# Layer 0 of a graph network: one tile in eight made by selection on TensorE instead of gathered by GpSimd

## The chip, the core and the metric

One core of a Trainium2 chip. The metric is the device time of one launch in microseconds; a kernel's time is the median of its runs. All times below of single instructions, waits and stretches come from one profiled execution.

## What is computed

A graph network of two layers on 12,500 nodes with 32 features and 212,500 edges, which are sorted by destination. Layer 0 is the part that the change touches:

```python
h = jnp.maximum(_layernorm(x, axis=-1), 0.0)
# layer 0
norm_src = rsqrt(maximum(deg_out, 1.0)); norm_dst = rsqrt(maximum(deg_in, 1.0))
h = features * norm_src[:, None]
msgs = h[src]
agg = segment_sum(msgs, dst) * norm_dst[:, None]
x = x + relu(agg @ weight + bias)
# layer 1: messages of h[src], a small network of edge_attr_32 and edge_attr_4, segment_sum over dst
```

`h[src]` is the row of 32 floats of the source node of every edge.

## The kernel before

The edges are padded to 208 chunks of 1024, a chunk being 8 tiles of 128 edges (one edge per partition). A row of a node's features is fetched by its index: one indirect DMA of GpSimd (L350) gathers the 128 rows of one tile from a table in DRAM into `g[:, j, t, 0:32]`. The tile `g` is a ring of four chunks (`RING` = 4, slot `j`); `idx` holds the indices of four chunks, which SP reloads once a slot's gather has landed (`load1`).

**Start.** Source digits are turned into one-hot tiles by VectorE (L738, bf16) and counted by 16 bf16 matmuls per batch on TensorE (L499), between one lone matmul at L493 and one at L505; that is the histogram, which gives the degrees. Meanwhile GpSimd gathers the raw rows of x for the first 32 chunks (the early chunks), which ScalarE keeps in SBUF (L406). Then VectorE makes layer 0's table `hn` (normalised rows times the norm), and ScalarE's queue stores it as `table1`. VectorE then makes the bounds of each chunk: the first destination row and the span of rows, in `row_i`.

**First stage of layer 0** (`beside_early`, 16 iterations). Six units alternate by the table `UNITS`: gathered, gathered, early, gathered, gathered, early. So four chunks gathered from `table1` and two early chunks are worked in an iteration. In both kinds of unit VectorE compares destinations into a one-hot tile (L783), TensorE multiplies it with the eight tiles of rows into a window of 68 destination rows (`take`, L515: eight fp32 matmuls, which the trace shows as 16 records), and VectorE adds the window to the accumulator `acc_a` (L795). TensorE's take number n waits until VectorE's take number n - 1 has added (the semaphore `opened`, L875 in VectorE's queue). Before an early chunk, VectorE splits its sources into digits and compares them (`early_onehots`, L830, L833, L835, then L840 to L847 on the rows kept), TensorE selects the norms with eight fp32 matmuls (`early_norms`, L537), and VectorE picks and applies them (`early_rows`, L856, L860, L862).

The order within a unit is written out by hand. VectorE: digits of the next unit if that is an early one, one-hot of the next unit, early rows if this is an early unit, then the addition of this unit's take. TensorE: norms if the next unit is early, wait for this unit's rows, take.

**Second stage** (`alone`, 28 iterations of four gathered chunks): one-hot of the next chunk, take of this one, and where destinations of a block of 512 nodes are complete, `mid_block` finishes the block (25 in all). GpSimd may gather into a slot again when the one-hot tile two units after the slot's use has been made (`used_in`).

**Layer 2 stage.** From 2205 us on, the second layer: gathers of all 208 chunks from `table2` run beside a long chain of matmuls and products (L605, L617, L982 to L1007). Its order is not touched.

Of the kernel before, what the change touches and what calls it, by code (L numbers as in the profile page):

```python
# [26 lines left out]
ALU = mybir.AluOpType  # L27
# [36 lines left out]
MW = 56  # L64


def gnn_program(nc, x_rows, src_all, src_chunks, src_rows, dst_all, dst_chunks, edge_t, sh_chunks,
# [3 lines left out]
    with ExitStack() as ctx:  # L71
# [11 lines left out]
        W_BANK, H_BANK, S_BANK = 0, 4, 6  # L83
# [10 lines left out]
        bound = sb("bound", [P, 2, CHUNKS])  # L94
# [16 lines left out]
        ident = sb("ident", [P, P])  # L111
        w_l0_s = sb("w_l0_s", [FEAT + 1, FEAT + 1])
# [22 lines left out]

        dst_i, src_i, src_p, src_b, src_r = (acc_a[:, k * T_ALL:(k + 1) * T_ALL].bitcast(I32) for k in range(5))
# [9 lines left out]
        early_r = early_r_all[:, 0:TILES * NR].rearrange("p (t r) -> p t r", r=NR)  # L146
        flat_q = q[:, :, :, :].rearrange("p b t k -> p (b t k)")
# [28 lines left out]
        mid_ready = sem("mid_ready")  # L176

# [76 lines left out]
        GATH = 16 * TILES  # L254
# [5 lines left out]
        def _(sp):  # L260
# [19 lines left out]
            def load1(i):  # L280
                for j in range(RING):

                    sp.wait_ge(gathered[j], GATH * (i + 1))
                    sp.dma_start(idx[:, j, :], load_from(src_chunks, RING * i + RING + j)).then_inc(idx_in[j], 16)

            def load_from(dram, c):
                return dram[c] if isinstance(c, int) else dram[bass.ds(c, 1)].rearrange("a p k -> (a p) k")

            with sp.Fori(0, EARLY_ITERS - 1) as i:
                load1(i)  # L290
# [9 lines left out]
            with sp.Fori(EARLY_ITERS - 1, ITERS - 1) as i:  # L300
                load1(i)

            for j in range(RING):
                sp.wait_ge(gathered[j], GATH * ITERS)
                sp.dma_start(idx[:, j, :], src_chunks[j]).then_inc(idx_in[j], 16)
                sp.dma_start(sh[:, j, :, :], sh_chunks[j].rearrange("p (t d) -> p t d", d=4)).then_inc(sh_in[j], 16)
# [10 lines left out]
            with sp.Fori(0, ITERS - 1) as i:  # L317
                final = final_blocks(sp, RING * i + (LOOK - 1))
                for j in range(RING):
# [4 lines left out]
                    sp.wait_ge(gathered[j], GATH * (i + ITERS + 1))  # L324
# [11 lines left out]
        def _(pool):  # L336
# [5 lines left out]
            def gather(i, table, iteration, free):  # L342

                for j in range(RING):
# [4 lines left out]
                    for t in range(TILES):  # L349
# [24 lines left out]
            gather(EARLY_ITERS, table1, EARLY_ITERS, kept_four_before)  # L374
            beside = used_in(0, len(UNITS), [UNITS.index((0, j)) for j in range(RING)])
            alone = used_in(A_UNITS, RING, range(RING))
            with pool.Fori(0, A_ITERS) as i:
                gather(i, table1, i + (EARLY_ITERS + 1), beside(i))
            with pool.Fori(0, REG_ITERS - A_ITERS - 1) as i:
                gather(i, table1, i + (EARLY_ITERS + 1 + A_ITERS), alone(i))  # L380
# [15 lines left out]
        def _(act):  # L396
# [60 lines left out]
            def coefs(i, j):  # L457
# [4 lines left out]
                act.wait_ge(gathered[j], GATH * (i + ITERS + 1))  # L462
# [24 lines left out]
        def _(pe):  # L487
# [52 lines left out]

            def beside_early(i):
                for pos, (is_early, k) in enumerate(UNITS):
# [4 lines left out]
                    else:  # L547
                        if UNITS[(pos + 1) % len(UNITS)][0]:
                            early_norms(2 * i + UNITS[pos + 1][1])
                        pe.wait_ge(gathered[k], GATH * (i + (EARLY_ITERS + 1)))  # L550
                        take(n, RING * i + (EARLY + k), k, pos % 2, lambda t: g[:, k, t, :])

            def alone(i):
                for j in range(RING):
                    pe.wait_ge(gathered[j], GATH * (i + (EARLY_ITERS + 1)))
# [15 lines left out]
            pe.wait_ge(acc_a_clear, 1)  # L571
            beside_early(0)
# [3 lines left out]
            with pe.Fori(A_ITERS, REG_ITERS) as i:  # L576
                alone(i)
            other_blocks(pe, blocks1, mid_block)
# [83 lines left out]
        def _(dve):  # L662
# [53 lines left out]
            for iota, m in ((iota_p, P), (iota_r, NR)):  # L716
# [12 lines left out]
                                          op0=ALU.bitwise_and, op1=ALU.bitwise_or))  # L729
            link(dve.tensor_copy(dig_p, src_p))  # L730
# [13 lines left out]
            with dve.Fori(1, HBATCH // 2) as i:  # L744
# [9 lines left out]
                                     op0=ALU.max, op1=ALU.mult).then_inc(table1_ready, 1)  # L754

# [69 lines left out]

            def early_onehots(e):
# [50 lines left out]
            def beside_early(i):  # L877

                for pos, (is_early, k) in enumerate(UNITS):
# [6 lines left out]
                    if is_early:  # L886
                        early_rows(2 * i + k)
                    take(len(UNITS) * i + pos, 2 * i + k if is_early else RING * i + (EARLY + k), pos % 2)

            def alone(i):  # L890
                for j in range(RING):
                    if not (isinstance(i, int) and j == RING - 1):
                        make_onehot(RING * i + (EARLY + j + 1), 1 - j % 2, onehot1_ready)
                    if j == LOOK:
# [46 lines left out]

            make_onehot(EARLY, 0, onehot1_ready)
            beside_early(0)
# [192 lines left out]
```

## Time and profile before

| | |
|---|---|
| median of 3 runs | 4374.91 us (4372.59 to 4389.63) |
| profiled execution, its own time | 4370.72 us |
| its span, first to last instruction | 4368.9 us |
| busy: TensorE / VectorE / ScalarE / GpSimd | 68% / 64% / 16% / 76% |
| mean granted TensorE clock | 0.77 |
| first take of a gathered chunk | 403.6 us |
| first stage / second stage / layer 2 | 403.6 to 1069.5 / to 2181.4 / 2205 to the end |

The granted clock is 1.00 at 2.4 GHz and 0.50 at 1.2 GHz. A gather is listed with its busy time; the rest of its spacing stands as "issue", time in which the engine waited for nothing that the profile shows.

### The profile page before, as it was taken

The page shows a single profiled execution, that of the slowest core. Times are in us where ns is not written, and L with a number is a line of the kernel's source. Part 1 is how long each engine was busy: PE and PEld are TensorE (multiplying, and loading weights), DVE is VectorE, ACT ScalarE, POOL GpSimd, SP SyncE. Part 2 cuts the span into 40 slices and gives each one's busy share as a digit, 9 for nine tenths or more (in the row PEclk, how much of TensorE's full clock was granted, in tenths as well). Part 3 has the DMA queues.
Part 4 walks back from the last instruction along what each step waited for, and adds up shares of the span by engine and source line. Part 5 has one row for each costly group of instructions (what it writes and reads, how often), then busy time and mean ns, then how long its engine had stood idle before and what let it go on. Part 6 is the DMA issues. An engine that isn't in the chain of part 4 may idle for free.

```text
span 4368.9 us, 66165 instructions
## 1 busy us (share of the span) xinstructions
PE 2966.2 (68%) x17022; PEld 2220.1 (51%) x17023; DVE 2776.1 (64%) x4667; ACT 718.6 (16%) x2399; POOL 3313.5 (76%) x3337
## 2 busy tenths in 40 slices
PE   6993444444222222222279999999999999999998
PEld 5772344434222222211256666666666666666666
DVE  7775444343222222211179999999999999899997
ACT  0000000000000000000043333333333333233322
POOL 7777777777777777777777777777777777777775
PEclk9999655555555555555599999999999999899998
DMA  2002111111111010110111111111111111111111
GB/s 51 11 11 44 37 37 42 37 37 28 15 15 15 15 15 15 15 14 14 15 27 29 29 29 28 29 29 28 29 29 27 29 28 28 27 29 29 27 29 19
DMA packets 224085, 113.80 MB, mean 26 GB/s; under 512 B 148848, under 2 KB 212145, under 8 KB 223953
## 3 DMA queue, kind: packets, MB, share of 16 engines
q0 software_dynamic: 106496, 54.74, 8.6%
q1 hardware_dynamic: 106281, 39.22, 4.0%
q10 hardware_dynamic: 11280, 19.53, 1.4%
q8 instruction: 10, 0.16, 0.0%
q14 instruction: 18, 0.15, 0.0%
HBM read 108.30 MB, written 4.92 MB: 26 GB/s over the span
## 4 chain that ended last, share of the span: by engine, by line
POOL 61%; issue 23%; PE 6%; DVE 5%; DMA 2%; ACT 1%; DVEq 1%; POOLq 1%; SPq 0%; ACTq 0%
POOL g L350 61%; PE ps L515 2%; DMA g<-table,idx 2%; PE ps L567 1%; PE ps L617 1%; PE ps L605 1%; ACT q L466 1%; DVE onehot L783 1%; ACT acc_b L445 0%; DVE prod_b L982 0%; PE ps L651 0%; DVE hn L936 0%; PE ps L653 0%; DVE ef L919 0%; ACT root L429 0%
## 5 line engine op out<-in xcount | busy, mean ns | idle before, releaser
L350 POOL DMA_INDIRECT g<-table,idx x3072 | 2990.3, 973 | 945.9 <-issue 924.2
L515 PE MATMUL ps<-onehot,g 128*33 128x68 f32 x2816 | 352.3, 318 | 986.3 <-issue 954.2
L617 PE MATMUL ps<-w_s,hid 128*128 128x256 f32 x3328 | 899.7, 417 | 2.0 <-DVE prod_a L993 1.4
L617 PEld LDWEIGHTS ps<-w_s,hid 128*128 128x128 f32 x3328 | 643.9, 204 | 454.9 <-issue 368.0
L515 PEld LDWEIGHTS ps<-onehot,g 128*33 128x33 f32 x2816 | 309.3, 174 | 1026.7 <-issue 998.4
L998 DVE TENSOR_REDUCE msg_b<-prod_b 128x128 f32<-128x1024 f32 x416 | 828.4, 1991 | 0.0
L795 DVE TENSOR_TENSOR acc_a<-acc_a,ps 33x68 f32 (+1 forms) x416 | 90.3, 217 | 1106.9 <-PE ps L515 1081.5
L605 PE MATMUL ps<-ef,w_s 32*64 32x512 f32 x832 | 482.6, 662 | 6.4 <-issue 6.3
L454 ACT ACTIVATE hid<-ps,b_s 64x512 f32<-64x512 f32 x416 | 282.2, 678 | 1118.2 <-PE ps L605 1117.8
L515 PEld LDWEIGHTS ps<-onehot,prod_a 128*128 128x128 f32 x3328 | 400.6, 193 | 119.4 <-issue 111.9
L515 PE MATMUL ps<-onehot,prod_a 128*128 128x68 f32 x3328 | 407.4, 276 | 77.4 <-issue 67.5
L466 ACT ACTIVATE q<-g,sh 128x32 f32<-128x32 f32 x1664 | 374.6, 308 | 330.8 <-DMA g<-table,idx 330.5
L982 DVE TENSOR_TENSOR prod_b<-ps,q 128x768 f32<-128x768 f32 x416 | 394.7, 949 | 20.5 <-PE ps L617 20.5
L350 POOL DMA_INDIRECT g<-x_rows,idx x256 | 309.8, 1210 | 80.1 <-issue 77.7
L783 DVE TENSOR_TENSOR onehot<-iota_all,dst_rel 128x544 f32<-128x544 f32 x416 | 300.1, 722 | 61.6 <-issue 53.3
L499 PE MATMUL ps<-acc_b 128*128 128x100 bf16 x1664 | 313.6, 370 | 33.4 <-DVE acc_b L738 33.4
L429 ACT ACTIVATE root<-stat 128x4 f32<-128x4 f32 x50 | 10.3, 205 | 1796.3 <-DVEq L689 1796.3
L499 PEld LDWEIGHTS ps<-acc_b 128*128 128x128 bf16 x1664 | 246.3, 148 | 100.4 <-DVE acc_b L738 33.6
L993 DVE TENSOR_TENSOR prod_a<-ps,q 128x512 f32<-128x512 f32 x416 | 283.6, 682 | 0.0
L515 PE MATMUL ps<-onehot,msg_b 128*56 128x68 f32 x3328 | 250.6, 231 | 0.0
L515 PEld LDWEIGHTS ps<-onehot,msg_b 128*56 128x56 f32 x3328 | 219.0, 134 | 15.1
L738 DVE TENSOR_TENSOR acc_b<-prod_a,msg_b 128x2048 bf16<-128x2048 bf16 x104 | 127.5, 1226 | 90.9 <-PE ps L499 90.9
(108 smaller groups left out, 1885.0 us busy)
## 6 DMA issues: line engine op xcount, KB each, us to landing
g<-table,idx POOLq DMA_INDIRECT x3072
ef<-edge_t SPq DMA_DIRECT2D x208, 128.0 KB
ef<-src_rows ACTq DMA_DIRECT2D x31, 512.0 KB, 3.7
idx<-src_chunks SPq DMA_DIRECT2D x416, 4.0 KB
g<-x_rows,idx POOLq DMA_INDIRECT x256
sh<-sh_chunks SPq DMA_DIRECT2D x208, 16.0 KB
table<-hn ACTq DMA_DIRECT2D x1, 1600.0 KB, 9.1
table<-hn ACTq DMA_DIRECT2D x25, 64.0 KB, 1.6
```

The costliest lines, as they stand in the source:

```text
L350: pool.indirect_dma_start(out=g[:, j, t, 0:FEAT], out_offset=None, in_=table, in_offset=bass.IndirectOffsetOnAxis(ap=idx[:, j, t:t + 1], a ...
L454: act.activation(hid[0:HID, h, :], ps[0:HID, H_BANK + h, :], ACT.Relu, bias=b1_s[:, 0:1]).then_inc(hidden_ready, 1)
L466: act.activation(q[:, j % 2, t, 8:40], g[:, j, t, 0:FEAT], ACT.Copy, scale=sh[:, j, t, 0:1])
L499: mm = pe.matmul(deg, oh_p[:, b, :, t], oh_r[:, b, :, t], start=False, stop=False, skip_group_check=True)
L515: mm = pe.matmul(ps[0:m, S_BANK + b, col:col + WIN], r, oh(t), start=(t == 0), stop=(t == TILES - 1))
L605: pe.matmul(ps[0:HID, H_BANK + h, :], w1_s[32 * j:32 * j + 32, :], ef[32 * j:32 * j + 32, 512 * h:512 * h + 512], start=True, stop=True, t ...
L617: mm = pe.matmul(w_ps[h][:, t, :], hid[:, h, P * t:P * t + P], w2_s[:, :], start=True, stop=True)
L738: ins = dve.tensor_tensor(oh[:, b, :, :], iota, dig[:, None, bass.ds(n * HB, HB)].to_broadcast([P, m, HB]), ALU.is_equal)
L783: dve.tensor_tensor(onehot[:, b, :, :], iota_all[:, None, 0:WIN].to_broadcast([P, TILES, WIN]), dst_rel[:, bass.ds(c * TILES, TILES)][:, : ...
L982: dve.tensor_tensor(prod_b[:, h, :, 0:3, :].rearrange("p t m (i o) -> p t m i o", o=MUL), w[:, :, 128:192].rearrange("p t (i o) -> p t i o ...
L993: dve.tensor_tensor(prod_a[:, b, 4 * h:4 * h + 4, :].rearrange("p t (k o) -> p t k o", o=MUL), w[:, :, 0:128].rearrange("p t (k o) -> p t ...
L998: dve.tensor_reduce(msg_b[:, b, 4 * h:4 * h + 4, 0:32].rearrange("p t (g o) -> p t g o", o=MUL), prod_b[:, h, :, :, :].rearrange("p t g (i ...
```

## The change

In layer 0, tile 7 of each of the 176 chunks that are gathered from `table1` is no longer gathered. GpSimd issues seven indirect DMAs per chunk there (`TAKEN` = 7); the 32 early chunks and layer 2 keep eight. The eighth tile is made as follows.

- Once, after the table is stored: SP loads `table1` back into SBUF as `whole` (node n lies on partition (n / 16) mod 128, in group n / 2048, at place n mod 16), and VectorE splits it into three bf16 parts whose sum is exact (`split`).
- Per chunk, SP loads the tile's 128 source indices, broadcast to all partitions (`load_key`, 64 KB). VectorE shifts them right by 4 (`key`) and compares them with the partition and group numbers into a bf16 one-hot tile of 7 x 128 columns (`make_source`).
- TensorE multiplies this with the three parts, 7 groups x 3 parts = 21 bf16 matmuls of 512 columns, into one PSUM bank (`source_rows`): for each edge the 16 rows that share its upper digits.
- VectorE picks the one of 16 (`choose`: a comparison with the low digit times the rows, 512 elements, then a sum over 16) and writes it to `g[:, j, 7, 0:32]`.

The one-hot tile of chunk m + 2 and the selection of chunk m + 1 are made in unit m. The tile `bound` and the third part lie in free space of `xc`, the semaphore targets count seven gathers in layer 0's stages, and constants are made at the start.

```diff
@@ gpsimd @@
-            def gather(i, table, iteration, free):
+            def gather(i, table, iteration, free, tiles=TILES):
...
-                    for t in range(TILES):
+                    for t in range(tiles):
...
-            gather(EARLY_ITERS, table1, EARLY_ITERS, kept_four_before)
+            gather(EARLY_ITERS, table1, EARLY_ITERS, kept_four_before, TAKEN)
...
@@ sync @@
+            def load_key(c, j):
+                row = src_rows[c:c + 1, MADE * P:] if isinstance(c, int) else src_rows[bass.ds(c, 1), MADE * P:]
+                sp.dma_start(keys[:, j, :], row.to_broadcast([P, P])).then_inc(keys_in[j], 16)
...
+                    sp.wait_ge(key_ready, RING * i + (j + 1))
+                    load_key(RING * i + (EARLY + RING + j), j)
...
+            load0(EARLY_ITERS - 1)
+            sp.wait_ge(table1_out, 16)
+            full = GROUPS - 1
+            sp.dma_start(whole[:, 0:full, :], table1[0:full * P * GROUP, :].rearrange(
+                "(k p b) f -> p k (b f)", p=P, b=GROUP)).then_inc(whole_in, 16)
...
@@ tensor @@
+            def source_rows(m, j):
+                if isinstance(m, int) and m >= M_UNITS:
+                    return
+                pe.wait_ge(source_ready, m + 1)
+                wait(pe, row_made, m - 1)
+                for k in range(GROUPS):
+                    for n in range(3):
+                        mm = pe.matmul(ps[:, R_BANK + j % 2, :], source[:, j % 2, k, :], split[n][:, k, :],
+                                       start=(k == 0 and n == 0), stop=(k == GROUPS - 1 and n == 2))
+                mm.then_inc(rows_psum, 1)
...
                         if UNITS[(pos + 1) % len(UNITS)][0]:
                             early_norms(2 * i + UNITS[pos + 1][1])
-                        pe.wait_ge(gathered[k], GATH * (i + (EARLY_ITERS + 1)))
+                        source_rows(RING * i + (k + 1), k + 1)
+                        pe.wait_ge(gathered[k], landed1(i))
+                        pe.wait_ge(row_made, RING * i + (k + 1))
                         take(n, RING * i + (EARLY + k), k, pos % 2, lambda t: g[:, k, t, :])
...
@@ vector @@
+            def make_source(m, j):
...
+                dve.wait_ge(keys_in[j], 4 * m + (16 - 4 * j))
+                wait(dve, source_ready, m)
+                dve.tensor_scalar(key, keys[:, j, :], GROUP_LOG, None, ALU.logical_shift_right).then_inc(key_ready, 1)
+                dve.wait_ge(key_ready, m + 1)
+                dve.tensor_tensor(source[:, j % 2, :, :], key[:, None, :].to_broadcast([P, GROUPS, P]),
+                                  first[:, :, None].to_broadcast([P, GROUPS, P]),
+                                  ALU.is_equal).then_inc(source_ready, 1)
+            def choose(m, j, c):
...
+                dve.wait_ge(rows_psum, m + 1)
+                dve.scalar_tensor_tensor(
+                    out=chosen.rearrange("p f b -> p b f"),
+                    in0=iota_all[:, 0:GROUP, None].to_broadcast([P, GROUP, FEAT]), scalar=low[:, bass.ds(c, 1)],
+                    in1=ps[:, R_BANK + j % 2, :].rearrange("p (b f) -> p b f", f=FEAT),
+                    op0=ALU.is_equal, op1=ALU.mult).then_inc(chosen_ready, 1)
+                dve.wait_ge(chosen_ready, m + 1)
+                dve.tensor_reduce(g[:, j, MADE, 0:FEAT], chosen, AX, ALU.add).then_inc(row_made, 1)
+            def next_rows(i, j):
+                make_source(RING * i + (j + 2), j + 2)
+                choose(RING * i + (j + 1), j + 1, RING * i + (EARLY + j + 1))
...
                     if is_early:
                         early_rows(2 * i + k)
+                    else:
+                        next_rows(i, k)
                     take(len(UNITS) * i + pos, 2 * i + k if is_early else RING * i + (EARLY + k), pos % 2)
...
+            dve.wait_ge(whole_in, 32)
+            link(dve.tensor_copy(split[0], whole))
+            link(dve.tensor_tensor(whole, whole, split[0], ALU.subtract))
+            link(dve.tensor_copy(split[1], whole))
+            dve.tensor_tensor(split[2], whole, split[1], ALU.subtract).then_inc(split_ready, 1)
```

How the order moves, first on TensorE, in the second gathered unit of an iteration (its next unit is an early one). Before, from the norms to the take (`hid` holds the early digits' one-hot, `row_i` the bounds):

```order
L537 MATMUL ps<-norm_src,hid 128x100 [waits early_p_ready]
L537 MATMUL ps<-norm_src,hid 128x100 x7
L521 TENSOR_LOAD row_i [waits onehot1_ready,gathered1]
...
L515 MATMUL ps<-onehot,g 33x68 [waits opened0]
L515 MATMUL ps<-onehot,g 33x68 x7
```

With the change (`prod_a` holds the source one-hot tile, `split_s` and `xc` the three parts):

```order
L599 MATMUL ps<-norm_src,hid 128x100 [waits early_p_ready]
L599 MATMUL ps<-norm_src,hid 128x100 x7
L611 MATMUL ps<-split_s,prod_a 128x512 [waits row_made,source_ready]
L611 MATMUL ps<-split_s,prod_a 128x512
L611 MATMUL ps<-xc,prod_a 128x512
...
L583 TENSOR_LOAD row_i [waits onehot1_ready,row_made,gathered1]
...
L577 MATMUL ps<-onehot,g 33x68 [waits opened0]
L577 MATMUL ps<-onehot,g 33x68 x7
```

The 21 matmuls for the next gathered chunk stand between the norms and the take, so the take of this chunk is queued behind them. The second place is VectorE in the same unit, from the last of the early digits' operations to the addition. Before:

```order
L847 TENSOR_TENSOR q<-q 128x256 [waits early_chain]
L783 TENSOR_TENSOR onehot<-iota_all,dst_rel 128x544
L799 TENSOR_LOAD row_i
...
L795 ISA [waits added1,seg1_done]
L795 TENSOR_TENSOR acc_a<-acc_a,ps 33x68
```

With the change:

```order
L966 TENSOR_TENSOR q<-q 128x256 [waits early_chain]
L870 TENSOR_TENSOR onehot<-iota_all,dst_rel 128x544
L920 TENSOR_SCALAR prod_a<-prod_a 128x128 [waits source_ready,keys_in3]
L922 TENSOR_TENSOR prod_a<-prod_a,first 128x896 [waits key_ready]
L932 SCALAR_TENSOR_TENSOR prod_a<-iota_all,low,ps 128x16x32 [waits rows_psum]
L938 TENSOR_REDUCE g<-prod_a 128x32 [waits chosen_ready]
L886 TENSOR_LOAD row_i
...
L882 ISA [waits added1,seg1_done]
L882 TENSOR_TENSOR acc_a<-acc_a,ps 33x68
```

The addition of this unit's take, and with it everything of the next unit, now stands behind a selection that waits for TensorE's 21 matmuls (`rows_psum`).

## Rows read from the trace of the kernel before

**Rows 1.** The page: busy times, clock in 40 slices, chain that ended last by line.

```profile
PE 2966.2 (68%) x17022; PEld 2220.1 (51%) x17023; DVE 2776.1 (64%) x4667; ACT 718.6 (16%) x2399; POOL 3313.5 (76%) x3337
PEclk9999655555555555555599999999999999899998
POOL g L350 61%; PE ps L515 2%; DMA g<-table,idx 2%; PE ps L567 1%; PE ps L617 1%; PE ps L605 1%; ACT q L466 1%; DVE onehot L783 1%; ACT acc_b L445 0%; DVE prod_b L982 0%; PE ps L651 0%; DVE hn L936 0%; PE ps L653 0%; DVE ef L919 0%; ACT root L429 0%
```

**Rows 2.** Table by stages: us, each engine's busy us (instructions), granted clock, DMA share, GB/s.

```profile
403.60:1069.50 665.90, 308.94 (x2049) 277.66 (x2049) 277.64 (x543) 0.00 (x0) 509.70 (x513) 0.57 0.16 38
1069.50:2181.40 1111.90, 273.81 (x1968) 243.33 (x1968) 241.00 (x846) 9.86 (x48) 842.21 (x887) 0.50 0.10 15
2205.00:4369.00 2164.00, 2062.63 (x11305) 1447.37 (x11304) 1971.80 (x2991) 691.05 (x2311) 1628.41 (x1664) 0.93 0.15 28
```

**Rows 3.** Timeline of GpSimd, second stage: start us, us, engine, line, operation [idle before].

```profile
1499.79 0.94 POOL L350 DMA_INDIRECT g<-table,idx  x1 [0.30 <-issue]
```

**Rows 4.** Timeline of TensorE: the first takes of the two stages.

```profile
403.63 2.02 PE L515 MATMUL ps<-onehot,g 128*33 128x68 f32 x16 [54.60 <-issue]
1069.49 2.02 PE L515 MATMUL ps<-onehot,g 128*33 128x68 f32 x16 [0.87 <-DVEq L875]
```

**Rows 5.** Timeline, first stage: half an iteration on TensorE and VectorE.

```profile
664.35 2.02 PE L515 MATMUL ps<-onehot,g 128*33 128x68 f32 x16 [2.53 <-issue]
666.59 0.22 DVE L795 TENSOR_TENSOR acc_a<-acc_a,ps 33x68 f32 x1 [5.71 <-PE ps L515]
671.46 2.02 PE L515 MATMUL ps<-onehot,q 128*33 128x68 f32 x16 [5.09 <-issue]
674.33 2.02 PE L515 MATMUL ps<-onehot,g 128*33 128x68 f32 x16 [0.85 <-DVEq L875]
678.53 3.74 PE L537 MATMUL ps<-norm_src,hid 128*128 128x100 f32 x16 [2.18 <-DVE hid L833]
```

**Rows 6.** Groups by line, shapes apart, one late addition, one DMA: prices for added operations.

```profile
L835 DVE TENSOR_TENSOR msg_b<-iota_all,acc_b 128x800 f32<-128x800 f32 x32 | 31.5, 984 | 0.0
L843 DVE TENSOR_REDUCE q<-q 128x8 f32<-128x256 f32 x32 | 13.4, 420 | 1.1
L993 DVE TENSOR_TENSOR prod_a<-ps,q 128x512 f32<-128x512 f32 x416 | 283.6, 682 | 0.0
1535.69 0.22 DVE L795 TENSOR_TENSOR acc_a<-acc_a,ps 33x68 f32 x1 [1.06 <-issue]
table<-hn ACTq DMA_DIRECT2D x1, 1600.0 KB, 9.1
```

**Rows 7.** The histogram: its matmuls, the lone ones before and after, a gather beside it.

```profile
304.70 20.52 PE L499 MATMUL ps<-acc_b 128*128 128x100 bf16 x108
L493 PE MATMUL ps<-acc_b 128*128 128x100 bf16 x1 | 0.3, 264 | 1.7 <-DVE acc_b L711 1.7
L505 PE MATMUL ps<-acc_b 128*128 128x100 bf16 x1 | 0.3, 263 | 0.0
310.52 1.44 POOL L350 DMA_INDIRECT g<-x_rows,idx  x1 [0.30 <-issue]
```

**Rows 8.** Layer 2, a fall and a rise of the clock: stretches, and TensorE's timeline there.

```profile
2406.70:2410.10 3.40, 3.40 (x16) 3.36 (x16) 3.40 (x5) 0.00 (x0) 2.49 (x4) 1.00 0.08 11
2410.10:2420.30 10.20, 10.20 (x19) 5.25 (x20) 6.94 (x11) 3.21 (x11) 7.76 (x9) 0.50 0.16 28
2420.30:2430.00 9.70, 9.70 (x62) 7.18 (x60) 7.93 (x15) 3.21 (x11) 7.34 (x8) 1.00 0.17 35
2399.86 1.99 PE L617 MATMUL ps<-w_s,hid 128*128 128x256 f32 x8
2404.81 1.15 PE L515 MATMUL ps<-onehot,msg_b 128*56 128x68 f32 x16
2407.10 0.63 PE L651 MATMUL ps<-sel_a_s,hn 128*128 128x32 f32 x2
2411.84 3.78 PE L617 MATMUL ps<-w_s,hid 128*128 128x256 f32 x8
```

More of the change, by code:

```diff
@@ L111, in gnn_program @@
         ident = sb("ident", [P, P])
+        split_s = sb("split_s", [P, 2, GROUPS, GROUP * FEAT], BF16)
+        low = sb("low", [P, CHUNKS])
+        first = sb("first", [P, GROUPS])
         w_l0_s = sb("w_l0_s", [FEAT + 1, FEAT + 1])
@@ L299, in _ @@
                 sp.dma_start(bound[:, k, :], bounds[k:k + 1, :].to_broadcast([P, CHUNKS])).then_inc(bounds_in, 16)
-            with sp.Fori(EARLY_ITERS - 1, ITERS - 1) as i:
+            sp.wait_ge(whole_clear, 1)
+            for j in range(RING):
+                load_key(EARLY + j, j)
+            load0(EARLY_ITERS - 1)
[3 more added lines that the diff above has]
+                "(k p b) f -> p k (b f)", p=P, b=GROUP)).then_inc(whole_in, 16)
+            sp.dma_start(whole[0:(NODES - full * P * GROUP) // GROUP, full, :], table1[full * P * GROUP:, :].rearrange(
+                "(p b) f -> p (b f)", b=GROUP)).then_inc(whole_in, 16)
+            with sp.Fori(0, REG_ITERS - 1) as i:
                 load1(i)
             for j in range(RING):
-                sp.wait_ge(gathered[j], GATH * ITERS)
+                sp.wait_ge(gathered[j], landed1(REG_ITERS - 1))
                 sp.dma_start(idx[:, j, :], src_chunks[j]).then_inc(idx_in[j], 16)
@@ L377, in _ @@
             with pool.Fori(0, A_ITERS) as i:
[L378 removed]
+                gather(i, table1, i + (EARLY_ITERS + 1), beside(i), TAKEN)
             with pool.Fori(0, REG_ITERS - A_ITERS - 1) as i:
[L380 removed]
+                gather(i, table1, i + (EARLY_ITERS + 1 + A_ITERS), alone(i), TAKEN)
             pool.wait_ge(added1, A_UNITS)
@@ L575, in _ @@
             pe.wait_ge(par_loaded, 16 * N_PARAMS)
-            with pe.Fori(A_ITERS, REG_ITERS) as i:
+            with pe.Fori(A_ITERS, REG_ITERS - 1) as i:
                 alone(i)
+            alone(REG_ITERS - 1)
             other_blocks(pe, blocks1, mid_block)
@@ L729, in _ @@
                                           op0=ALU.bitwise_and, op1=ALU.bitwise_or))
+            link(dve.tensor_scalar(low_i, src_i.rearrange("p (c t) -> p c t", t=TILES)[:, :, MADE],
+                                   GROUP - 1, None, ALU.bitwise_and))
+            link(dve.tensor_copy(low[:, :], low_i))
+            for k in range(GROUPS):
+                link(dve.tensor_scalar(first[:, k:k + 1], part[:, :], float(P * k), None, ALU.add))
             link(dve.tensor_copy(dig_p, src_p))
```

69 lines of the change are left out of this document (61 added, 8 removed).

## The prediction

> **What bounds the kernel now.** The page first: GpSimd is busy 76% and its gather at L350 makes 61% of the chain that ended last, with 23% "issue" beside it [rows 1]. The table by stages then tells three stages apart [rows 2]: 403.6 to 1069.5 us, where layer 0's gathered chunks and the 32 early chunks alternate; 1069.5 to 2181.4, gathered chunks alone; and layer 2, where TensorE is busy 2063 of 2164 us and which the edit leaves as it is. In the first two TensorE and VectorE are busy less than half of the time. GpSimd issues a gather every 1.25 us, 0.94 busy and 0.30 "issue" [rows 3], so a chunk of eight costs 10.0 us. The first stage took (1069.49 - 403.63) / 16 = 41.6 us per iteration of four gathered and two early chunks [rows 4], a little over its 32 gathers (40 us). Both stages are bound by GpSimd. That is the case for the change. The case against it is in the order of the work on the other two engines.
>
> **What GpSimd saves.** 176 chunks lose one gather of 1.25 us: at most 220 us, 80 of it in the first stage (64 chunks) and 140 in the second (112), if the seven that are left still bound each chunk.
>
> **What a made tile costs.** TensorE: 21 matmuls (7 groups, 3 parts) of 512 bf16 columns, each with 128 columns of weights. No row shows that shape. The histogram's matmuls are bf16 with 100 columns and 128 of weights: 108 in 20.52 us, 190 ns each, 0.83 ns per column if weights count as columns [rows 7]. At which clock? The page's line of 40 slices prints full speed up to 437 us [rows 1], but the very first matmul and the lone one that ends the histogram, of one shape, took 264 and 263 ns [rows 7], and the take at 403.63, also under a printed 9, took the same 2.02 us as the one at 1069.49, where the printed clock is 0.50 [rows 2, 4]. So I read 0.83 ns as the column at 1.2 GHz and 0.42 at 2.4. Bounds: all weights hidden, 21 x 512 x 0.83 = 8.9 us at 1.2 GHz and 4.5 at 2.4; none hidden, 21 x 640, 11.2 and 5.6. I take the middle, 10.1 and 5.1. The Trainium skill ("TensorE: Matmul & The Clock Gate", section on the back-to-back issue gap) gives 427 and 216 ns for such a matmul in a stream, with the next weights pulled ahead: 9.0 and 4.5 us, by which an iteration below would be about 2.5 us shorter when warm and 4.5 when cold. In the histogram rows the weights were not hidden.
> VectorE: a shift of 128 elements, about 0.17 us; the comparison of 896, by the 800 of L835 in 0.98, about 1.10; the selection of 512 out of PSUM, by L993, 0.68; the reduction of 512, on the line from L843 (256 in 0.42) to L835, 0.69 [rows 6]. Together 2.64 us, 2.9 with gaps. Its share is no bound (278 busy of 666 us before, [rows 2]); its place in the queue matters.
> SP: one more DMA of 64 KB per chunk, behind a wait for the shift, which ran two units before: nothing, as the slot's next use is three chunks away. The bounds tile in xc and the constants made once: nothing.
>
> **The chain in the first stage.** An iteration is two halves of three units: gathered, gathered, early. Walk a half from the start of its second gathered take [rows 5]: take at 664.35, its sum added at 666.59, one-hot and early rows, take of the early chunk at 671.46 (7.1 us on); the next gathered take at 674.33; its sum, then the integer digits of the next early chunk, and the norms' matmuls at 678.53 (4.2 us on). Nothing of this ran beside the other: TensorE waits for VectorE and VectorE for TensorE, and only because 20 us of gathers lie under each half was it free. The change puts TensorE's 21 matmuls ahead of each gathered take, and VectorE's selection (which waits for them) ahead of the addition of that take. So the 21 matmuls for the next chunk begin only when the take before them is done, and the digits, norms and early rows only after selection, take and addition. After the matmuls VectorE has 0.17 to hear of it, 1.5 for selection and reduction and 1.06 for loading the bounds (the idle time before an addition that comes late, [rows 6]), 2.7 us in place of the 2.24 from take to addition: both waits grow by 0.5 us. A half is then, in order: 7.6 (matmuls' end to early take) + early take + 21 matmuls + 4.7 (to the norms) + norms + 21 matmuls.
> - At 1.2 GHz: 7.6 + 2.0 + 10.1 + 4.7 + 3.7 + 10.1 = 38.2 us, 76.4 per iteration. Takes and norms by [rows 5].
> - At 2.4 GHz: 7.6 + 1.1 + 5.1 + 4.7 + 1.9 + 5.1 = 25.5, 51.0 per iteration. The take is by the 1.15 of 16 records at a granted 1.00 [rows 8]; the norms are half of 3.74.
> Either is more than the 35 us of 28 gathers, and more than 41.6: the gathers stop bounding this stage.
>
> **The clock.** L617's eight records took 1.99 us at a granted 1.00 and 3.78 at 0.50 [rows 8]. In layer 2 the clock fell after a stretch of narrow matmuls, 32 columns to 128 of weights, and TensorE then worked 10.2 us without a pause at half clock before it rose [rows 8]. In the new half TensorE idles 7.6 - 1.1 = 6.5 us and 4.7 - 1.1 = 3.6 us. I expect the clock to fall at each and to rise within the dense matmuls behind it, after some 8.5 us (a little under the row's 10.2). Work done at half clock for 8.5 us costs 4.25 us more, twice a half: 25.5 + 8.5 = 34.0, 68.0 us per iteration. Against 41.6: +26.4 x 16 = **+422 us**.
>
> **The second stage.** Here TensorE has per chunk the 21 matmuls and a take, 6.2 us at 2.4 GHz and 12.1 at 1.2, and no early work; the selection for the next chunk lies beside the wait for the gather. Where TensorE falls behind it has no pause and the clock rises, so it keeps to seven gathers, 8.75 us. VectorE's operations in the histogram stretched gathers to 1.44 us [rows 7]; bf16 goes out of the comparison too. I take 0.15 us per chunk, 8.9 in all; ends 0 and 0.65 (one stretched gather and some of the next). 10.0 - 8.9 = 1.1, x 112 = **-123 us**; ends -140 and -67. The Trainium skill ("SBUF — State Buffer", its rules for DVE and GpSimd) says that tensor_tensor has no two-port mode and, as an inference, does not hold up descriptor generation; by it the comparison would stretch nothing. The rows of the histogram, where VectorE runs nothing but such operations, speak otherwise.
>
> **Start and seam.** Before, the first take is at 403.63. Now SP loads the table (1.6 MB, by the store's 9.1 us [rows 6]) after the last x gathers, to about 404; four operations of 3584 elements follow, two at 3.9 (the slope between L843 and L835, 1.04 ns per element), two conversions at perhaps 2.2: 12.2 us, 416; matmuls 10.1 (cold), selection 1.7, comparison 1.3, matmuls 10.1: first take at about 440, **+37 us**. At the seam to the second stage the ring of four lies full, about three chunks ahead: **-25 us**.
>
> **Sum:** +37 + 422 - 123 - 25 = +311. The profiled execution took 4370.7 us (span 4368.9), so 4682; the median of three runs is 4.2 us higher than it: **4686 us**, slower by 7%. With 4.5 us matmuls and a low clock for only a third of the row's 10.2 us behind each pause, a half is 27.7 us, the stage +221 and the end 4468. With 5.6 us matmuls and the clock mostly low, a half is 40.1, the stage +618 and the second -67: 4938.
>
> **Rivals.**
> - *The clock stays at 2.4 GHz in the pauses.* For it: pauses of 3.6 us are not much, and the matmuls are dense. Against: in the first stage TensorE was busy 309 of 666 us and had 0.57. The stage is +150: 4375 + 29 = 4404. Decides: full clock in takes of early chunks.
> - *The clock never rises.* For it: 300 us of uninterrupted bf16 matmuls in the histogram did not raise it, as I read the 263 ns. Against: there 100 columns stood to 128 of weights; here 512. First stage 16 x 34.8 = +557; the second is then bound by TensorE at 12.1 + 1.2 = 13.3 us per chunk, +370: 5339.
> - *Faster: the gathers bound both stages.* The place is the half: if its chain takes less than 17.8 us, two chunks of seven gathers, it is hidden. That needs VectorE's selection and TensorE's matmuls to overlap the early chunk's steps, which the queues forbid as I read them, and full clock. Then 176 x 1.1 = -194 and 20 at the start: about 4200.
> - *It does not do what it says*: the order on GpSimd has seven gathers per chunk, so no.
>
> **How the numbers follow.** My case 0.63, full clock 0.15, never 0.10, gathers bound 0.08, the rest (TensorE late in the second stage, something unseen) 0.04. The range holds mine and the full clock: 4400 to 4900. About 0.5%, 22 us, can be told from no change. The full-clock case straddles that line: 0.06 of it goes to "same", with 0.01 more of the others; faster 0.09; slower 0.84.
>
> **What would show it.** First stage about 1090 us from first take to the end of the alternation, 65 to 72 per iteration, GpSimd idle there for want of a free slot; second stage 8.8 to 9.2 per chunk; 21 matmuls in 4.5 to 11.2 us; granted clock in the first stage between 0.6 and 0.8; the first take near 440. Wrong, if an iteration takes under 45 us, or if gathers still follow each other every 1.25 us there.

## The result and the profile after

| | before | after |
|---|---|---|
| median of four runs, us | 4378.1 (4372.6 to 4389.6) | 4597.3 (4596.4 to 4604.7) |
| profiled execution: time, span | 4370.7, 4368.9 | 4604.7, 4602.9 |
| first take | 403.6 | 430.2 |
| first stage, per iteration | 665.9, 41.6 | 979.3, 61.2 |
| second stage, to the last take | 1116.9 | 1001.5 |
| rest of the span | 2182.6 | 2191.9 |

The change makes the kernel slower: ratio 1.050, 95% interval 1.049 to 1.052 (a second set of runs of the same two kernels: 1.050, 1.048 to 1.053). By the table the spans differ by +26.6 + 313.4 - 115.4 + 9.3 = +234 us. The loss is in the first stage, and the second gains. The last 9.3 us lie in layer 2, which the change leaves as it is: this rest took 2187.0 us in another profiled execution of the changed kernel and 2184.6 to 2190.9 in three kernels of the experiments, so much of the 9.3 is the spread of single executions.

Some of the experiments below ran on chips on which the kernels, the one before too, took 36 to 38% longer, with pauses ("stalls" below) that the traces do not explain; there only ratios and stages of the same set are compared.

The page of the kernel after, against [rows 1]: busy times, granted clock in 40 slices, the chain that ended last by engine.

```profile
PE 3788.5 (82%) x20570; PEld 2489.5 (54%) x20719; DVE 3317.7 (72%) x5385; ACT 718.4 (16%) x2399; POOL 3191.8 (69%) x3161
PEclk9999777777778888888889999899999999999998
POOL 48%; issue 21%; PE 20%; DVE 7%; DVEq 2%; ACT 1%; DMA 1%; POOLq 0%; SPq 0%; ACTq 0%
```

GpSimd had 61% of the chain by its gather alone; now TensorE and VectorE hold 27% of it. The stages say where (columns as in [rows 2]; the second stage runs to the start of its last take):

```profile
430.20:1409.50 979.30, 614.82 (x3330) 378.87 (x3394) 470.74 (x800) 0.00 (x0) 445.99 (x454) 0.72 0.12 29
1409.50:2411.00 1001.50, 778.91 (x4197) 407.28 (x4279) 568.40 (x1285) 9.86 (x48) 758.41 (x757) 0.85 0.14 21
```

In the first stage no engine is busy for more than 63% of the time, and GpSimd for 46%, where it had 77% [rows 2]. Its waits there, then one such wait in its timeline:

```profile
POOL g L412 <- DVE onehot L870: 400.4, 59, 11.8
...
POOL g L412 <- issue: 130.7, 395, 4.1
```

```profile
803.77 1.30 POOL L412 DMA_INDIRECT g<-table,idx  x1 [11.12 <-DVE onehot L870]
```

It waits 400 us for a free slot: the one-hot of a later chunk, which tells it that a slot has been used, comes late. Half an iteration on TensorE and VectorE (the counterpart of [rows 5]; L599 are the norms, L611 the 21 matmuls, L577 takes, L882 additions, L932 and L938 selection and its sum):

```profile
800.18 3.74 PE L599 MATMUL ps<-norm_src,hid 128*128 128x100 f32 x16 [3.98 <-DVE hid L952]
...
804.14 0.63 PE L611 MATMUL ps<-split_s,prod_a 128*128 128x512 bf16 x1 [0.22 <-issue]
...
809.42 1.13 PE L577 MATMUL ps<-onehot,g 128*33 128x68 f32 x16
809.64 1.08 DVE L932 SCALAR_TENSOR_TENSOR prod_a<-iota_all,low,ps 128x512 f32<-128x512 f32 x1 [5.39 <-PE ps L611]
...
812.54 0.22 DVE L882 TENSOR_TENSOR acc_a<-acc_a,ps 33x68 f32 x1 [1.10 <-issue]
...
817.40 2.02 PE L577 MATMUL ps<-onehot,q 128*33 128x68 f32 x16 [6.85 <-issue]
...
819.76 0.63 PE L611 MATMUL ps<-split_s,prod_a 128*128 128x512 bf16 x1 [0.33 <-issue]
...
825.75 1.14 PE L577 MATMUL ps<-onehot,g 128*33 128x68 f32 x16
...
828.99 0.22 DVE L882 TENSOR_TENSOR acc_a<-acc_a,ps 33x68 f32 x1 [1.22 <-issue]
...
830.95 1.39 PE L599 MATMUL ps<-norm_src,hid 128*128 128x100 f32 x5 [4.06 <-DVE hid L952]
```

From norms to norms it is 30.8 us, one step behind the other, as the prediction had laid the chain out. The clock in that half, stretch by stretch:

```profile
800.10:806.10 6.00, 5.70 (x22) 4.41 (x24) 4.01 (x9) 0.00 (x0) 2.03 (x2) 0.52 0.33 101
806.10:812.90 6.80, 4.45 (x32) 2.33 (x30) 1.98 (x3) 0.00 (x0) 4.94 (x6) 0.99 0.08 12
812.90:823.00 10.10, 5.26 (x24) 3.11 (x26) 5.33 (x9) 0.00 (x0) 6.61 (x7) 0.50 0.10 15
823.00:830.90 7.90, 3.89 (x29) 2.05 (x27) 3.44 (x6) 0.00 (x0) 0.00 (x0) 0.93 0.04 7
```

It falls in each of TensorE's two pauses, and 5.7 and 5.3 us of work are done at 1.2 GHz before it is back at 2.4.

### The profile page after: what moved, and what is told of

It reads as the page before. It is cut to its first block, busy times and chain, and to the rows that moved or that the text cites. A ratio compares the mean times of both kernels' runs of the same rounds, so it can differ in the third digit from the quotient of the medians.

```text
span 4602.9 us, 75819 instructions
## 1 busy us (share of the span) xinstructions
PE 3788.5 (82%) x20570; PEld 2489.5 (54%) x20719; DVE 3317.7 (72%) x5385; ACT 718.4 (16%) x2399; POOL 3191.8 (69%) x3161
## 4 chain that ended last, share of the span: by engine, by line
POOL 48%; issue 21%; PE 20%; DVE 7%; DVEq 2%; ACT 1%; DMA 1%; POOLq 0%; SPq 0%; ACTq 0%
POOL g L412 48%; PE ps L611 8%; PE ps L577 4%; PE ps L698 3%; PE ps L599 3%; DVE prod_a L932 2%; PE ps L686 2%; DVEq L887 1%; DVEq L886 1%; DVE prod_b L975 1%; DVE q L979 1%; DMA g<-table,idx 1%; DVE hid L952 1%; ACT q L528 1%; DVE prod_b L949 0%
## 5 line engine op out<-in xcount | busy, mean ns | idle before, releaser
L412 POOL DMA_INDIRECT g<-table,idx x2896 | 2868.2, 990 | 1300.3 <-issue 867.4
L611 PE MATMUL ps<-split_s,prod_a 128*128 128x512 bf16 x2316 | 828.8, 439 | 138.9 <-DVE prod_a L922 115.3
L611 PE MATMUL ps<-xc,prod_a 128*128 128x512 bf16 x1232 | 527.0, 428 | 1.5
L611 PEld LDWEIGHTS ps<-split_s,prod_a 128*128 128x128 bf16 x2464 | 260.9, 111 | 467.2 <-issue 220.0
L577 PE MATMUL ps<-onehot,prod_a 128*128 128x68 f32 x3328 | 407.9, 276 | 83.9 <-issue 76.7
L577 PEld LDWEIGHTS ps<-onehot,prod_a 128*128 128x128 f32 x3328 | 400.0, 193 | 127.7 <-issue 120.7
L932 DVE SCALAR_TENSOR_TENSOR prod_a<-iota_all,low,ps 128x512 f32<-128x512 f32 x176 | 188.9, 1073 | 376.2 <-PE ps L611 375.7
L882 DVE TENSOR_TENSOR acc_a<-acc_a,ps 33x68 f32 (+1 forms) x416 | 89.9, 216 | 385.5 <-PE ps L577 228.3
L577 PE MATMUL ps<-onehot,g 128*33 128x68 f32 x2816 | 217.5, 235 | 123.0 <-issue 109.7
L577 PEld LDWEIGHTS ps<-onehot,g 128*33 128x33 f32 x2816 | 186.3, 118 | 200.6 <-issue 200.6
```

Of the source, the lines that this page charges most:

```text
L412: pool.indirect_dma_start(out=g[:, j, t, 0:FEAT], out_offset=None, in_=table, in_offset=bass.IndirectOffsetOnAxis(ap=idx[:, j, t:t + 1], a ...
L577: mm = pe.matmul(ps[0:m, S_BANK + b, col:col + WIN], r, oh(t), start=(t == 0), stop=(t == TILES - 1))
L611: mm = pe.matmul(ps[:, R_BANK + j % 2, :], source[:, j % 2, k, :], split[n][:, k, :], start=(k == 0 and n == 0), stop=(k == GROUPS - 1 and ...
L932: dve.scalar_tensor_tensor(out=chosen.rearrange("p f b -> p b f"), in0=iota_all[:, 0:GROUP, None].to_broadcast([P, GROUP, FEAT]), scalar=l ...
```

## Experiments

**The made tile in the second stage alone.** The first stage gathers eight tiles again; the three bf16 parts are formed at the seam.

```diff
 GpSimd: with pool.Fori(0, A_ITERS - 1) as i:
-            gather(i, table1, i + (EARLY_ITERS + 1), beside(i), TAKEN)
+            gather(i, table1, i + (EARLY_ITERS + 1), beside(i))
 TensorE, beside_early:
-            source_rows(RING * i + (k + 1), k + 1)
...
-            pe.wait_ge(row_made, RING * i + (k + 1))
...
 VectorE, behind beside_early:
...
+            link(dve.tensor_copy(split[0], whole))
...
+            choose(0, 0, EARLY + RING * A_ITERS)
```

> The made tile in the second stage alone: the 80 chunks up to the end of the alternation with early chunks gather eight tiles as before, the 112 chunks behind it gather seven and have the eighth made; the three parts are formed at the seam between the stages. Theory A (the loss is the chain of TensorE and VectorE in the alternating first stage, and only that): the first stage goes back to about 41.6 us per iteration and the first take to about 404, the second stage keeps its 9.0 us per chunk; 4378 - 115 plus 0 to 15 for the parts formed at the seam = 4263 to 4280, faster than before. Rival B (the made tile costs something wherever it is, and the second stage shows a gain only because the first left the ring of gathered chunks full): second stage at 9.6 or more per chunk, 4330 or more. Rival C (loading the whole table beside the rest is part of the loss): first stage over 43 us per iteration.

Measured: 5931 us beside 6019, ratio 0.986 (0.981 to 0.991). The ratio has theory A's sign, but the times were those of none of the theories: one iteration of the first stage, the same code as before, took 58 us instead of 41.6. VectorE's timeline there:

```profile
763.79 0.42 DVE L988 SCALAR_TENSOR_TENSOR q<-q 128x256 f32<-128x256 f32 x1
776.91 0.22 DVE L889 TENSOR_TENSOR acc_a<-acc_a,ps 33x68 f32 x1 [12.70 <-remote]
```

The instructions last as long as ever; two to three times per iteration VectorE stands still for 10 us or so, for a reason that the trace calls "remote" or "issue". The same kernel was run on two other chips.

> The same kernel as in the first run, since on that chip every kernel, the one before too, took 37% longer than in the profiles of before and after. The expectation stands: theory A, second stage 9.0 us per chunk, first stage as before, 0.972 to 0.978 of the kernel before (4263 to 4280 us beside 4378). Rival B: second stage 9.6 or more per chunk, 0.99 or more. In the first run's trace the engines stood still for 10 us and more at the ends of loops; if that is how every chip behaves and not that chip's state, this run shows about 0.986 and 5930 us again.

Measured on another such chip: 5916 beside 6030, 0.981 (0.977 to 0.985). The second stage took 12.8 us per chunk.

> The kernel of the first and fifth run once more, wanted on a chip like that of the profiles. Theory A there: first take at 404 to 406, 41.4 us per iteration in the first stage, second stage 9.0 us per chunk with 0 to 15 us at the seam: 4255 to 4280, 0.972 to 0.978 of the kernel before, and 5 to 25 us under the run with the other order. Rival B: 4330 or more. On a chip like that of the first eight runs 0.981 to 0.986 again.

Measured on a chip like that of the profiles: 4285.5 beside 4380.4, ratio 0.979 (0.976 to 0.981), without stalls. The stages:

```profile
403.90:1067.10 663.20, 308.46 (x2048) 277.05 (x2048) 277.29 (x542) 0.00 (x0) 507.52 (x511) 0.57 0.16 38
1067.10:2099.00 1031.90, 802.88 (x4335) 412.95 (x4336) 586.26 (x1299) 9.86 (x48) 787.43 (x776) 0.84 0.14 21
```

The first stage is back at 41.4 us per iteration and the kernel is faster than before. Theory A stands. Rival C falls (41.4 us against over 43), and so does B's price (9.2 us per chunk against 9.6 or more). But 9.2 is not the 9.0 of theory A either: the 9.0 of the kernel after held a ring that its slow first stage had left full (28 us, worked out below), and this part of rival B is so. The time came 5 us above the range, and beside the run with the other order (4282, below) where 5 to 25 us less had been expected. At the seam, VectorE and GpSimd:

```profile
1067.31 2.54 POOL L419 DMA_INDIRECT g<-table,idx  x1 [0.30 <-issue]
1067.70 2.03 DVE L1075 CAST split_s<-acc_b 128x3584 bf16<-128x3584 f32 x1 [0.35 <-DVE acc_a L889]
1069.76 3.89 DVE L1076 TENSOR_TENSOR acc_b<-acc_b,split_s 128x3584 f32<-128x3584 f32 x1
1070.15 5.68 POOL L419 DMA_INDIRECT g<-table,idx  x1 [0.30 <-issue]
1073.69 2.03 DVE L1077 CAST split_s<-acc_b 128x3584 bf16<-128x3584 f32 x1
1075.75 3.89 DVE L1078 TENSOR_TENSOR xc<-acc_b,split_s 128x3584 bf16<-128x3584 f32 x1
1076.14 4.32 POOL L419 DMA_INDIRECT g<-table,idx  x1 [0.30 <-issue]
```

Three gathers take 12.5 us in place of 2.8 while the parts are formed: 9.7 us, within the 0 to 15 that had been expected at the seam. Without them a chunk takes 9.1 us. In the kernel after, the same four operations stretch three gathers at 401 to 414 us.

**The saving without the work.**

> The kernel before with one gather per chunk left out in both layer-0 stages, and nothing in its place (the eighth tile of a chunk keeps older rows). It gives what GpSimd alone can save. Theory A: second stage 8.8 us per chunk, nothing stretched by new VectorE work, 112 x 1.25 = -140; first stage 28 x 1.25 = 35.0 us per iteration if its own chain is shorter than that, 37 if not, -75 to -105: 4135 to 4165. Rival B (the second stage's 9.0 is a limit other than GpSimd's): second stage stays at 9.0 or more here too.

Measured on a chip with stalls: 5806 beside 6019, 0.967 (0.961 to 0.973), 213 us. Its stages, 54 us per iteration and 12.2 per chunk, hold the stalls. Theory A's 8.8 us per chunk can't be seen at that level, so this run leaves the question against rival B open.

**The work without the saving.**

> The changed kernel with all eight gathers kept; the made rows go to a tile that nobody reads. It is the cost without the saving. Theory A: in the first stage the chain is the bound, 61.2 us per iteration with 28 gathers and as much with 32, which need 40; the second stage goes back to 10.0 to 10.2 us per chunk: 4378 + 27 + 313 + 0 to 15 = 4718 to 4735. Rival D (in the first stage the gathers still carry part of the time, since each chunk waits for its last one): the first stage grows by 3 us or more per iteration, over 4770.

Measured on the same chip: 6243, ratio 1.036 (1.031 to 1.041). In the second stage it took 1555 us. Two kernels with seven gathers and the same work there took 1442 (the made tile in the second stage alone, with its seam) and 1420 (the other order, below) on this chip: 1.0 to 1.2 us per chunk, so there the gather counts. Its first stage (68.5 us per iteration) can't be held against 61.2, since no time of the change itself exists from such a chip. So rival D is neither shown nor excluded.

**The same work in another order, first stage.** TensorE takes before it multiplies; VectorE selects behind the early chunk's rows, or behind the one-hot of the unit.

```diff
 TensorE:
-                        source_rows(RING * i + (k + 1), k + 1)
                         pe.wait_ge(gathered[k], landed1(i))
                         pe.wait_ge(row_made, RING * i + (k + 1))
                         take(n, RING * i + (EARLY + k), k, pos % 2, lambda t: g[:, k, t, :])
+                        source_rows(RING * i + (k + 1), k + 1)
...
 VectorE:
                     if is_early:
                         early_rows(2 * i + k)
+                        after = UNITS[pos - 1][1] + 1
+                        choose(RING * i + after, after, RING * i + (EARLY + after))
                     else:
-                        next_rows(i, k)
+                        if not UNITS[pos - 1][0]:
+                            choose(RING * i + k, k, RING * i + (EARLY + k))
+                        make_source(RING * i + (k + 2), k + 2)
```

> The changed kernel with the same work in the first stage in another order: TensorE takes a gathered chunk before it multiplies for the next one, and VectorE selects behind the addition or behind the early chunk's rows, so that the 21 matmuls lie beside VectorE's work. Theory A (the place in the queues makes the chain): an iteration falls from 61.2 us to 44 to 52, 4597 - 150 to 275 = 4320 to 4450, middle 4360. Rival E (the amount of the added work, at the clock it gets, is the bound, whatever its place): 57 or more per iteration, 4530 or more.

> The same kernel as in the fourth run, on this chip. Theory A (the place in the queues makes the chain): 44 to 52 us per iteration in the first stage in place of 61.2, 0.987 to 1.016 of the kernel before, middle 0.996. Rival E (the amount of the added work is the bound, whatever its place): 57 or more per iteration, 1.035 or more.

Measured, both with stalls: 5962 and 5952, ratios 0.989 (0.982 to 0.995) and 0.986 (0.983 to 0.990). The ratios are at the good end of theory A's, but the iteration (60 us, with stalls) can't be read against its 44 to 52.

The other order again, and with it the selection's product is written without a stride (its sum then reads with one):

```diff
-                    out=chosen.rearrange("p f b -> p b f"),
+                    out=chosen,
...
-                dve.tensor_reduce(g[:, j, MADE, 0:FEAT], chosen, AX, ALU.add).then_inc(row_made, 1)
+                dve.tensor_reduce(g[:, j, MADE, 0:FEAT], chosen.rearrange("p b f -> p f b"), AX, ALU.add).then_inc(row_made, 1)
```

> The first stage in the other order (take first, then the 21 matmuls; selection behind the addition or the early rows), and the selection's product written without a stride, its sum then read with one. Theory A: the selection falls from 1.08 us to 0.68 to 0.75 (L993 of the kernel before, the same operation without strides), the reduction stays at 0.69 or grows by up to 0.4; first stage as in the other-order runs or up to 1.5 us per iteration less. On a chip like that of those runs 0.980 to 0.990 of the kernel before; on one like that of the profiles 36 to 42 us per iteration, 4230 to 4330 us.

Measured on a chip like that of the profiles: 4282.5 beside 4375.7, ratio 0.978 (0.975 to 0.981). Stages, the two selection groups, and GpSimd's waits in the first stage:

```profile
424.10:1095.90 671.80, 511.37 (x3335) 315.01 (x3399) 468.20 (x801) 0.00 (x0) 470.66 (x454) 0.89 0.18 42
1095.90:2096.00 1000.10, 786.00 (x4228) 411.53 (x4308) 571.58 (x1289) 9.87 (x48) 758.68 (x763) 0.84 0.14 22
```

```profile
L938 DVE TENSOR_REDUCE g<-prod_a 128x32 f32<-128x512 f32 x176 | 179.7, 1021 | 6.0
L932 DVE SCALAR_TENSOR_TENSOR prod_a<-iota_all,low,ps 128x512 f32<-128x512 f32 x176 | 131.2, 745 | 169.3 <-PE ps L611 169.2
```

```profile
POOL g L412 <- DVE onehot L870: 68.8, 40, 4.3
```

With the same 21 matmuls per chunk an iteration fell from 61.2 to 42.0 us, and GpSimd waits 69 us for slots, not 400. The order made the chain; rival E falls. The stride did not matter: the product fell from 1.07 to 0.745 us, and the sum that now reads with the stride grew from 0.69 to 1.02, together 1.76 to 1.77 both times, and the second stage, where only the stride differs, took 1000.1 us in place of 1001.5. So the gain is the order's. The clock is part of it: with fewer pauses the granted clock of the stage was 0.89 in place of 0.72, and this run doesn't tell the two apart.

Against the kernel before, the first stage gains nothing by the made tile even so: 42.0 us per iteration beside 41.6. What makes this kernel faster than before is the second stage, and the kernel with the made tile there alone is as fast (4285.5).

**The clock.** TensorE's pauses are filled with matmuls that serve nothing.

```diff
+            def fill(count):
+                for n in range(count):
+                    pe.matmul(ps[:, H_BANK, :], split[0][:, 0, 0:P], split[0][:, 1, :], start=(n == 0),
+                              stop=(n == count - 1))
...
                         take(n, RING * i + (EARLY + k), k, pos % 2, lambda t: g[:, k, t, :])
+                        fill(28 if UNITS[(pos + 1) % len(UNITS)][0] else 14)
```

> The changed kernel with TensorE's two pauses in each half of an iteration filled: 28 matmuls of 512 columns into an unused PSUM bank behind the take ahead of an early chunk (6.0 us at the 0.216 us each that the profile after shows at full clock), 14 behind the other gathered take (3.0 us). They do nothing for the result and hold the queue for no longer than the pauses last. Theory A' (what the prediction priced as the clock's share): granted clock near 1 in the first stage, early take 1.1 in place of 2.0 us, norms 1.9 in place of 3.7, 21 matmuls 4.5 each: 51 to 54 us per iteration in place of 61.2, 4597 - 115 to 165 = 4430 to 4480. Rival F (the clock costs little, the waits on VectorE all): 59 or more per iteration, 4560 or more.

Measured with stalls: 6004, ratio 0.998 (0.995 to 1.002), 64 us per iteration. This is inconclusive: a stall is a pause that nothing fills.

> The kernel of the seventh run once more, for the price of the clock on a chip like that of the profiles, where the changed kernel needs 61.2 us per iteration in the first stage. Theory A' (cold matmuls, takes and norms behind the pauses are on the chain): 51 to 55 us per iteration, 4430 to 4500, early take 1.1 us and norms 1.9 us. Rival F (the clock costs little): 59 or more. A third outcome counts against the filling and not against A': if the 28 and 14 matmuls last longer than the pauses do (at half clock they take 12.0 and 6.0 us), the iteration stays near 60 though takes and norms are short.

Measured without stalls: 4430.1 beside 4380.4, ratio 1.013 (1.010 to 1.017). Its first stage, and the pieces that were cold before:

```profile
430.00:1234.00 804.00, 754.96 (x4717) 402.58 (x4716) 467.46 (x796) 0.00 (x0) 455.18 (x450) 1.00 0.15 35
```

```profile
802.13 1.13 PE L577 MATMUL ps<-onehot,q 128*33 128x68 f32 x16 [0.69 <-issue]
...
813.01 2.03 PE L599 MATMUL ps<-norm_src,hid 128*128 128x100 f32 x16 [0.92 <-DVE hid L958]
...
827.48 1.13 PE L577 MATMUL ps<-onehot,q 128*33 128x68 f32 x16 [0.70 <-issue]
```

The granted clock is 1.00, an iteration takes 50.3 us, and it is 25.35 from one early take to the next. More work made the kernel 164 us faster than the change alone: of the 19.6 us by which an iteration of the changed kernel is longer than before (61.2 against 41.6), the fallen clock costs 10.9, and the chain at full clock is the other 8.7. Rival F falls.

**One part instead of three.** The made rows are then rounded to bf16.

```diff
-                    for n in range(3):
+                    for n in range(1):
...
-                                       start=(k == 0 and n == 0), stop=(k == GROUPS - 1 and n == 2))
+                                       start=(k == 0 and n == 0), stop=(k == GROUPS - 1 and n == 0))
```

> The changed kernel with 7 matmuls for a made tile in place of 21: only the first of the three bf16 parts is used, the made rows are rounded to bf16. Everything else, VectorE's work and all waits too, stays. Per half of an iteration TensorE is spared 28 matmuls: 12.0 us at the 0.427 us each of the half clock, 6.0 at 0.216; the clock will be lower, since less dense work follows each pause. Theory A (matmuls lie on the chain, one for one): 61.2 - 12 to 16 = 45 to 49 us per iteration, 4340 to 4410; the second stage stays at 9.0. Rival F (the chain is VectorE's waits): 55 or more.

Measured with stalls: 5901, ratio 0.979 (0.974 to 0.983), 62 us per iteration. Neither expectation can be read at that level. The second stage took 11.8 us per chunk where the kernel with filled pauses, which has 21 matmuls there and ran on the same chip, took 12.7. No theory had this: TensorE was busy 486 of 1321 us there, and 862 of 1422 with 21 matmuls. Why 14 matmuls fewer save 0.9 us per chunk beside stalls stays open.

**The two kernels again.**

> The changed kernel itself, since on the chips of the first eight runs VectorE and TensorE stand still some 10 us twice per iteration and every kernel takes 37% longer than in the profiles of before and after. It gives what those eight are to be compared with. Theory A: where the chip is like that, the chain gets the stalls on top, so the changed kernel is slower than the kernel before by less than 5.0%: the run with the added work but no gather left out stood at 1.036, and the saving of the second stage is 1.2 us x 112 = 134 of 6020 us, 0.022: 1.010 to 1.020, 66 to 68 us per iteration in the first stage. If this chip is like the one of the profiles, 1.050 again.

Measured: 4593.9 beside 4375.7, 1.050 (1.048 to 1.053), without stalls. So the runs above that are said to be without stalls can be held against the profiles of before and after; there is no time of the changed kernel beside the stalls.

## Why the prediction was right

Forecast was +311 us on the profiled execution, measured +234; 4686 us against 4597, inside the range and with the right sign. The place of the loss and its cause, the chain through both queues, were forecast and shown. The total is closer than its terms: the start was put 10 us and the first stage 109 us too high, the second stage with its seam 33 us too low, and the 9 us of layer 2 were not forecast. By its terms:

- **The chain of a half iteration: right.** The forecast of 25.5 us at 2.4 GHz stood at 25.35 with the pauses filled. That it is so close is partly luck, two errors that cancel. The two sets of 21 matmuls take 9.3 us, not 10.2, and the two waits 13.2 us, not 12.3, mostly because the selection takes 1.07 us, not 0.68, in each; its sum of 0.69 was right. A matmul's weights are hidden: in the timeline of the kernel after the first three begin at 804.14, 804.57 and 804.99, 0.43 us apart, and warm ones follow each other every 0.216. The formulas of the Trainium skill ("TensorE: Matmul & The Clock Gate", section "Back-to-back issue gap") give the same 427 and 216 ns for 512 columns, and the trace agrees.
- **The clock: mechanism right, size wrong.** This is the mis-sized term, "work done at half clock for 8.5 us costs 4.25 us more, twice a half". The work done cold was 5.7 and 5.3 us, so 2.8 and 2.6, together 5.5 in place of 8.5 per half. Twice 3.0 times 16 is 96 of the 109 us by which the stage was overestimated (+422 against +313); the chain, 51.0 forecast against 50.3, is 11 of the rest. The row that it was taken from has a TensorE that works without a pause; here part of the slow stretch lies in the pause itself (10.1 us at 0.50, 5.3 of them busy). The price comes out the same from the filled pauses: (61.2 - 50.3) / 2 = 5.5.
- **Second stage and seam: forecast -123 - 25, measured -115.** 757 gathers in 1001.5 us are 108.1 chunks, and 111 takes were begun after the first, so the ring was three chunks ahead: 3 x 9.3 = -28 us, near the -25 of the forecast. But a chunk costs 1001.5 / 108.1 = 9.26 us, not 8.9: seven gathers of 1.00 busy (758.4 / 757) and 0.30 make 9.1, and waits for a slot (19.1 us) the rest. The term of 0.15 us per chunk for stretched gathers is 0.37 by their mean (1.002 against 0.949 [rows 2]), within its ends. The timeline shows one beside the comparison:

```profile
1799.43 1.09 DVE L922 TENSOR_TENSOR prod_a<-prod_a,first 128x896 bf16<-128x896 int32 x1
...
1799.61 1.73 POOL L412 DMA_INDIRECT g<-table,idx  x1 [0.30 <-DVE onehot L870]
```

- **Start: +26.6, forecast +37.** The four operations took the 12.2 us expected, from 400.9 us on in place of 404, and the matmuls warmed up within the first set. Its first matmuls, from 415.2 on, still begin 0.43 us apart where the profile prints a granted clock of 1.00: the prediction was right not to trust the print up to 437 us.
- **Rivals.** "The clock stays at 2.4 GHz" was priced at +150 for its stage; with the pauses filled it is 804.0 - 665.9 = +138. "The gathers bound both" named VectorE's selection and the early steps lying beside the matmuls as its condition: the other order does just that, and gave 4282 where about 4200 had been priced. The 80 us between them are those of the first stage, which was to gain 70 and lost 6: its gathers are stretched (454 of 1.04 us), and GpSimd waits 69 us.
- Of the signs that were named, the granted clock (0.72), GpSimd's waits for a free slot, the 9.0 us per chunk and the 4.5 us of warm matmuls held. The first stage took 979 us in place of 1090, 61 per iteration in place of 65 to 72, and the first take came at 430 in place of 440.

## What to carry to other kernels

Work moved off the bounding engine is paid at its place in the queues of the others: walk the chain that the queues make before adding up busy shares. Where two engines hand work back and forth, issue the step that somebody waits for first and the step for the next round behind it; here that order turned a loss of 5.0% into a gain of 2.2%. Then compare stage by stage with the kernel before: the whole gain came from the stage that had no early work, and the change was worth making there alone. Price a fallen clock by the busy time in the slow stretch, not by its length.

## What the runs showed of the hardware

- Some of VectorE's operations on SBUF hold up a gather that begins beside them. Beside 12 us of them on 3584 elements (two conversions, two subtractions) three gathers took 2.54, 5.68 and 4.32 us instead of 0.94; the comparison of 896 elements with a bf16 result stretched one to 1.73. In the kernel before, 69 gathers that began during a one-hot comparison of 544 f32 elements (0.72 us) took 1.20 on average. Not every operation does it: gathers that began beside the selection, which reads PSUM, or beside its sum took 0.94. The Trainium skill ("SBUF — State Buffer", section "Who interferes with whom") infers that tensor_tensor, which has no two-port mode, leaves descriptor generation alone. The trace does not agree: the gather that began at 1076.14, 0.4 us into a subtraction of 3.89 us, took 4.32 us and ended 0.8 us behind it.
- A strided side costs VectorE 0.33 us per 512 f32 elements, written or read: 1.07 and 0.69 became 0.745 and 1.02.
- Useless matmuls can pay: 42 of 0.216 us per half iteration, laid into TensorE's pauses, kept the granted clock at 1.00 and gave 164 us back.
- On some chips the same kernel took 5931 instead of 4286 us, its instructions as long as ever, with stalls of some 10 us two to three times per iteration on VectorE. What the engines wait for there stays open.
